# First attention of a hybrid block: two score buffers instead of three, four pairs of output banks instead of two, head weights applied after the normalisation, evictions issued ahead of exponents

## The reference

```python
logits = jnp.einsum('bhid,bhjd->bhij', q, k) * SCALE
logits = jnp.einsum('bhij,gh->bgij', logits, Wpre)
attn = jax.nn.softmax(logits, axis=-1)
attn = jnp.einsum('bhij,gh->bgij', attn, Wpost)
out = jnp.einsum('bhij,bhjd->bhid', attn, v)
```

## Time and profile before

| | |
|---|---|
| Median of 3 runs | 2481.05 us (2480.69 to 2481.33) |
| Profiled execution | 2480.47 us, its span 2478.7 us |
| Granted TensorE clock, mean over the span | 0.945 |
| Busy over the span | PE 89%, DVE 84%, ACT 74%, POOL 50% |
| First attention, first to last row maximum | 77.4 to 1488.9 us |
| 600 to 1000 us, busy | PE 387.36, DVE 368.22, ACT 347.33, POOL 191.12 us, PE clock 1.00 |

### The profile page before, as it was taken

How to read it: one execution, slowest core, us unless ns; L and a number is a source line. 1 busy time by engine, 2 the same in 40 slices (tenths; PEclk the granted TensorE clock), 3 DMA queues, 4 the chain that set the end, 5 groups by cost and what they waited for, 6 DMA issues and landing times. The chain is left out here.

```text
span 2478.7 us, 62316 instructions
## 1 busy us (share of the span) xinstructions
PE 2199.3 (89%) x22576; PEld 1502.2 (61%) x22576; DVE 2077.6 (84%) x3160; ACT 1822.4 (74%) x2674; POOL 1237.8 (50%) x1482
## 2 busy tenths in 40 slices
PE   5899999999999999999999994556899999999556
PEld 3466676666766676666766664443455555555544
DVE  6899999999999999999999995655799999997473
ACT  1788888888888888888888882115799998998002
POOL 3445444444444544445444452300788888887030
PEclk9999999999999999999999997669799999999866
DMA  2799999999999999999999993006222222222001
GB/s 93 121 196 187 196 187 192 191 192 189 194 189 194 184 197 192 190 189 192 192 189 191 192 194 71 1 8 207 70 69 72 70 69 70 70 69 51 29 1 34
DMA packets 1183691, 333.54 MB, mean 135 GB/s; under 512 B 1145968, under 2 KB 1174512, under 8 KB 1183216
## 3 DMA queue, kind: packets, MB, share of 16 engines
q1 hardware_dynamic: 1182320, 326.97, 74.2%
q10 hardware_dynamic: 1152, 3.62, 0.4%
HBM read 30.57 MB, written 14.68 MB: 18 GB/s over the span
## 5 line engine op out<-in xcount | busy, mean ns | idle before, releaser
L329 PE MATMUL a_out_ps<-a_vs,a_pT 128*128 128x129 f16 x4096 | 726.0, 221 | 48.4 <-ACT a_own_out L378 46.6
L416 DVE SCALAR_TENSOR_TENSOR a_parts<-a_probs,a_parts 128x1024 f16<-128x1024 f32 x512 | 653.2, 1276 | 115.1 <-ACT a_parts L369 115.1
L333 PE MATMUL a_out_ps<-a_vs,a_pT 128*128 128x129 f16 x4096 | 724.5, 219 | 0.0
L331 PE MATMUL a_out_ps<-a_vs,a_pT 128*128 128x128 f16 x4096 | 724.4, 218 | 0.0
L361 ACT ACTIVATE a_probs<-a_score_ps,a_negmax 128x1024 f32<-128x1024 f32 x512 | 571.8, 1117 | 164.9 <-DVE a_negmax L410 164.8
L410 DVE TENSOR_REDUCE a_negmax<-a_score_ps 128x1 f32<-128x1024 f32 x512 | 621.2, 1213 | 2.4 <-PE a_score_ps L315 2.4
L369 ACT ACTIVATE a_parts<-a_probs 128x1024 f16<-128x1024 f32 x512 | 543.5, 1061 | 0.6 <-DMA a_pT<-a_parts 0.6
L329 PEld LDWEIGHTS a_out_ps<-a_vs,a_pT 128*128 128x128 f16 x4096 | 396.4, 97 | 146.1 <-ACT a_own_out L378 99.1
L331 PEld LDWEIGHTS a_out_ps<-a_vs,a_pT 128*128 128x128 f16 x4096 | 402.9, 98 | 44.6
L477 POOL TENSOR_TENSOR acc<-acc,a_own_out 128x256 f32<-128x256 f32 x256 | 247.9, 969 | 352.3 <-DVE a_parts L416 346.4
L311 PE MATMUL a_score_ps<-kh,a_qs 128*128 128x512 f16 x1024 | 388.6, 379 | 10.3 <-DVE a_qs L401 7.0
(11 more groups left out here) (199 smaller groups left out, 2701.4 us busy)
## 6 DMA issues: line engine op xcount, KB each, us to landing
a_pT<-a_parts SPq DMA_TRANSPOSE x512, 5.0
b_qs<-q_parts SPq DMA_DIRECT2D x128, 64.0 KB, 2.0
b_ks<-k_parts SPq DMA_DIRECT2D x128, 64.0 KB, 1.9
q_parts<-b_parts SPq DMA_DIRECT2D x32, 128.0 KB, 1.9
k_parts<-b_parts SPq DMA_DIRECT2D x32, 128.0 KB, 1.9
v_parts<-b_v_all SPq DMA_DIRECT2D x4, 1024.0 KB, 4.6
b_vs<-v_parts SPq DMA_DIRECT2D x32, 128.0 KB, 2.1
b_sent_pT<-b_sent_parts SPq DMA_TRANSPOSE x256, 2.3
```

The costliest lines, as they stand in the source:

```text
L329: pe.matmul(out[:, 0:D + 1], hi, vs[:, G % 2, 0, j, 0:D + 1], start=j == 0, stop=False, skip_group_check=True)
L331: pe.matmul(out[:, 0:D], hi, vs[:, G % 2, 1, j, 0:D], start=False, stop=False, skip_group_check=True)
L333: last = pe.matmul(out[:, 0:D + 1], lo, vs[:, G % 2, 0, j, 0:D + 1], start=False, stop=j == JB - 1, skip_group_check=True)
L416: dve.scalar_tensor_tensor(out=parts[:, T % RING_P, 1, :], in0=probs[:, T % RING_P, :], scalar=PSCALE, in1=parts[:, T % RING_P, 0, :], op0 ...
```

## The change

Five things change in `attend_a`. The three score buffers become two, so `scores(T)` waits for the exponent of T - 2 in place of T - 3. The output banks go from two pairs to four, so `times_v(T)` waits for the eviction of tile T - 7 in place of T - 3. v is split into its parts once per batch instead of being scaled and split once per head, and POOL multiplies each evicted pair by `wpost` (`weigh`) and then adds it. ACT's `evict` stands ahead of the step's `exponentiate`, and DVE's `invert` ahead of its `row_max`. The addition of a pair follows the weighing of the next, and both stand at odd steps.

```diff
+        weighed = st.sb(s, "a_weighed", [P, 2, 2, D])
         qs = st.sb(s, "a_qs", [P, 2, 2, SEQ], F16)
-        vs = st.sb(s, "a_vs", [P, 2, 2, JB, D + 2], F16)
-        vtmp = st.sb(s, "a_vtmp", [P, JB, D])
-        score_ps = [st.ps(s, f"a_score_ps{i}", [P, SEQ]) for i in range(3)]
-        out_ps = st.ps(s, "a_out_ps", [P, 2, 2, 2 * D])
+        vs = st.sb(s, "a_vs", [P, NB, 2, JB, D + 2], F16)
+        score_ps = [st.ps(s, f"a_score_ps{i}", [P, SEQ]) for i in range(2)]
+        out_ps = st.ps(s, "a_out_ps", [P, 4, 2, 2 * D])
...
                 G, t = T // TPB, T % TPB
                 if t == 0:
                     pe.wait_ge(qlo_made, G + 1)
-                if T >= 3:
-                    pe.wait_ge(exp_done, T - 2)
-                out, base = score_ps[T % 3], G // HA * SEQ
+                if T >= 2:
+                    pe.wait_ge(exp_done, T - 1)
+                out, base = score_ps[T % 2], G // HA * SEQ
                 qhi, qlo = qs[:, G % 2, 0, t * P:(t + 1) * P], qs[:, G % 2, 1, t * P:(t + 1) * P]
...
             def times_v(T):
-                G, t = T // TPB, T % TPB
-                if t == 0:
-                    pe.wait_ge(vlo_made, G + 1)
-                if T >= 4 and T % 2 == 0:
-                    pe.wait_ge(evicted, T - 2)
+                b = T // (HA * TPB)
+                if T % (HA * TPB) == 0:
+                    pe.wait_ge(vlo_made, b + 1)
+                if T >= 8 and T % 2 == 0:
+                    pe.wait_ge(evicted, T - 6)
                 wait_turned(pe, T)
-                out = out_ps[:, T // 2 % 2, T % 2, :]
+                out = out_ps[:, T // 2 % 4, T % 2, :]
                 for j in range(JB):
                     hi, lo = pT[:, T % RING_T, 0, j, :], pT[:, T % RING_T, 1, j, :]
-                    pe.matmul(out[:, 0:D + 1], hi, vs[:, G % 2, 0, j, 0:D + 1], start=j == 0, stop=False,
+                    pe.matmul(out[:, 0:D + 1], hi, vs[:, b, 0, j, 0:D + 1], start=j == 0, stop=False,
-                    pe.matmul(out[:, 0:D], hi, vs[:, G % 2, 1, j, 0:D], start=False, stop=False,
+                    pe.matmul(out[:, 0:D], hi, vs[:, b, 1, j, 0:D], start=False, stop=False,
-                    last = pe.matmul(out[:, 0:D + 1], lo, vs[:, G % 2, 0, j, 0:D + 1], start=False,
+                    last = pe.matmul(out[:, 0:D + 1], lo, vs[:, b, 0, j, 0:D + 1], start=False,
                                      stop=j == JB - 1, skip_group_check=True)
                 last.then_inc(pv_done, 1)
...
                 act.wait_ge(max_ready, T + 1)
                 if T >= RING_P:
                     act.wait_ge(lo_ready, T - RING_P + 1)
-                act.activation(probs[:, T % RING_P, :], score_ps[T % 3][:], ACT.Exp,
+                act.activation(probs[:, T % RING_P, :], score_ps[T % 2][:], ACT.Exp,
                                bias=negmax[:, T % 8:T % 8 + 1]).then_inc(exp_done, 1)
             def high(T):
...
                 act.wait_ge(rden_ready, pair + 1)
                 if pair >= 2:
-                    act.wait_ge(added, pair - 1)
+                    act.wait_ge(weighed_ready, pair - 1)
                 for T in (2 * pair, 2 * pair + 1):
-                    act.activation(own_out[:, T % 4, :], out_ps[:, pair % 2, T % 2, 0:D], ACT.Copy,
+                    act.activation(own_out[:, T % 4, :], out_ps[:, pair % 4, T % 2, 0:D], ACT.Copy,
                                    scale=rden[:, pair % 2, T % 2:T % 2 + 1]).then_inc(evicted, 1)
             scale_q(0)
             scale_q(1)
             for i in range(TILES_A + AH + 2):
+                if i >= AH + 2 and i % 2 == 0:
+                    evict((i - AH - 2) // 2)
                 if i < TILES_A:
                     exponentiate(i)
-                if i >= AH + 2 and i % 2 == 0:
-                    evict((i - AH - 2) // 2)
                 if 1 <= i <= TILES_A:
                     high(i - 1)
                 if i % TPB == 1 and i < TILES_A:
...
                 dve.wait_ge(scored, T + 1)
                 if T >= 8:
                     dve.wait_ge(exp_done, T - 7)
-                dve.tensor_reduce(negmax[:, T % 8:T % 8 + 1], score_ps[T % 3][:], AX.X, ALU.max,
+                dve.tensor_reduce(negmax[:, T % 8:T % 8 + 1], score_ps[T % 2][:], AX.X, ALU.max,
                                   negate=True).then_inc(max_ready, 1)
             def low(T):
...
                 dve.wait_ge(pv_done, 2 * pair + 2)
                 if pair >= 2:
                     dve.wait_ge(evicted, 2 * pair - 2)
-                dve.reciprocal(rden[:, pair % 2, :], out_ps[:, pair % 2, :, D]).then_inc(rden_ready, 1)
+                dve.reciprocal(rden[:, pair % 2, :], out_ps[:, pair % 4, :, D]).then_inc(rden_ready, 1)
             low_q(0)
             low_q(1)
             for i in range(TILES_A + AH + 2):
+                if i >= AH + 2 and i % 2 == 0:
+                    invert((i - AH - 2) // 2)
                 if i < TILES_A:
                     row_max(i)
-                if i >= AH + 2 and i % 2 == 0:
-                    invert((i - AH - 2) // 2)
                 if 2 <= i < TILES_A + 2:
                     low(i - 2)
                 if i % TPB == 3 and TPB <= i < TILES_A:
...
                 if i >= 2:
                     pool.wait_ge(lo_ready, min(i - 1, TILES_A))
-            def scale_v(G, c):
-
-                if c == 0 and G >= 1:
-                    pool.wait_ge(vlo_made, G)
+            def high_v(b):
+
+                pool.tensor_scalar(vs[:, b, 0, :, 0:D], v[:, b * SEQ:(b + 1) * SEQ].rearrange("p (j d) -> p j d", j=JB),
+                                   1.0, 1.0, ALU.mult, ALU.mult).then_inc(vhi_made, 1)
+
+            def low_v(b, c):
+
+                pool.wait_ge(vhi_made, b + 1)
                 own = slice(c * JB // 2, (c + 1) * JB // 2)
-                src = v[:, (G // HA) * SEQ + c * HALF:(G // HA) * SEQ + (c + 1) * HALF]
-                w = wpost[:, (G % HA) * D:(G % HA + 1) * D][:, None, :].broadcast_to([P, JB // 2, D])
-                pool.tensor_tensor(vtmp[:, own, :], src.rearrange("p (j d) -> p j d", j=JB // 2), w,
-                                   ALU.mult).then_inc(v_scaled, 1)
-
-            def high_v(G):
-
-                pool.wait_ge(v_scaled, 2 * G + 2)
-                if G >= 2:
-                    pool.wait_ge(pv_done, TPB * (G - 1))
-                pool.tensor_scalar(vs[:, G % 2, 0, :, 0:D], vtmp[:], 1.0, 1.0, ALU.mult, ALU.mult).then_inc(vhi_made, 1)
-
-            def low_v(G, c):
-
-                pool.wait_ge(vhi_made, G + 1)
-                own = slice(c * JB // 2, (c + 1) * JB // 2)
-                last = pool.tensor_tensor(vs[:, G % 2, 1, own, 0:D], vtmp[:, own, :], vs[:, G % 2, 0, own, 0:D],
-                                          ALU.subtract)
+                src = v[:, b * SEQ + c * HALF:b * SEQ + (c + 1) * HALF]
+                last = pool.tensor_tensor(vs[:, b, 1, own, 0:D], src.rearrange("p (j d) -> p j d", j=JB // 2),
+                                          vs[:, b, 0, own, 0:D], ALU.subtract)
                 if c == 1:
                     last.then_inc(vlo_made, 1)
+            def weigh(pair):
+
+                pool.wait_ge(evicted, 2 * pair + 2)
+                if pair >= 2:
+                    pool.wait_ge(added, pair - 1)
+                g = 2 * pair // TPB % HA
+                w = wpost[:, g * D:(g + 1) * D][:, None, :].broadcast_to([P, 2, D])
+                slot = 2 * pair % 4
+                pool.tensor_tensor(weighed[:, pair % 2, :, :], own_out[:, slot:slot + 2, :], w,
+                                   ALU.mult).then_inc(weighed_ready, 1)
+
             def add(pair):
-                pool.wait_ge(evicted, 2 * pair + 2)
+                pool.wait_ge(weighed_ready, pair + 1)
                 at = (2 * pair // TPB // HA) * TPB + 2 * pair % TPB
-                slot = 2 * pair % 4
-                pool.tensor_tensor(acc[:, at:at + 2, :], acc[:, at:at + 2, :], own_out[:, slot:slot + 2, :],
+                pool.tensor_tensor(acc[:, at:at + 2, :], acc[:, at:at + 2, :], weighed[:, pair % 2, :, :],
                                    ALU.add).then_inc(added, 1)
             pool.memset(vs[:, :, 0, :, D:], 1.0).then_inc(ones_ready, 1)
+            high_v(0)
+            low_v(0, 0)
+            low_v(0, 1)
             pool.memset(acc[:], 0.0).then_inc(cleared, 1)
             pool.wait_ge(cleared, 1)
-            for i in range(TILES_A + AH + 4):
-                G, t = i // TPB, i % TPB
-                if i < TILES_A and t < 5:
+            for i in range(TILES_A + AH + 2):
+                b, step = i // (HA * TPB) + 1, i % (HA * TPB) - 3 * TPB
+                if b < NB and step in (0, 2, 4):
                     pace(i)
-                    if t in (0, 1):
-                        scale_v(G, t)
-                    elif t == 2:
-                        high_v(G)
+                    if step == 0:
+                        high_v(b)
                     else:
-                        low_v(G, t - 3)
```

(19 more changed lines are left out.)

## The result

The changed kernel takes 2453.45 us (median of 3 runs, 2450.41 to 2457.91), against 2481.05 before: a ratio of 0.989, 95% interval 0.987 to 0.991. It is 27.6 us faster. I had said 2435, 46 us faster, with 2425 to 2464 as the range. Its runs lie 7.5 us apart, where those of before lay 0.6 us apart.

A forecast was written before the change was run, and what follows sets the result against it. A DVE-ACT loop was taken to set the pace: 20.81 us plus 0.58 for POOL is 21.39 us a group, a gain of 0.76; times 62, less 2 us once, gives 45.1 off 2480.47: 2435 us, range 2425 to 2464.

The forecast's parts named there:

- my own forecast: The main case for the changed kernel: 21.28 to 21.55 us a group of eight tiles, 2423 to 2445 us; chance 0.52.
- full blocking: Rival: POOL and DVE fully block each other at low parts, 21.85 us a group, 2445 to 2464 us; chance 0.22.
- What bounds the kernel: A loop between DVE and ACT, not PE, sets the pace of about 22.15 us per group of eight tiles.
- Evictions and reciprocals ahead: ACT's and DVE's new order: no new wait for the reciprocal, 6.83 us through ACT, loop 20.81 us a group without POOL's effect.
- Weights on evicted outputs: POOL's weighing and adding slow DVE's low parts: 0.24 us at steps 6 and 8, 0.10 at step 4, 0.58 a group.
- Four output banks, two score buffers: PE's 0.70 us wait a group for evicted banks goes; neither part gains by itself, and score buffers leave no reserve.
- score buffers' rival: Score buffers bind: a late exponent 4 stalls PE each group, some 21.6 us a group, 2448 us; chance 0.12.
- Transposes: The DMA's landing of 5.0 us is hidden behind the about 7.8 us before a high part needs it.
- PE's floor: PE's own pace when left alone: 2.66 us a tile, 21.28 us a group.
- Once: One-time costs: third score's wait, v's parts beside the first `low_q`, one more POOL operation at the end; +2 us together.
- if high parts wait for DMAs: Sign of being wrong: ACT's high parts wait for the transposing DMAs; no size given.
- The two others: Signs of being wrong: score matmuls wait for exponents over 0.2 us a group; POOL's two operations take over 1.7 us a pair.

The follow-up runs named there:

- experiment 3: Only the banks changed (two score buffers, four pairs of output banks) on the kernel before: 2479.67 us, ratio 1.000.
- experiment 2: Only the order changed (evictions ahead of exponents, reciprocals ahead of row maxima) on the kernel before: 2545.15 us, ratio 1.027.
- experiment 4: Only v's parts made once per batch and the weights put on evicted outputs, on the kernel before: 2457.4 us, ratio 0.992.
- experiment 7: The changed kernel with only the high parts transposed, half the bytes per DMA: 2428.54 us, ratio 0.978, groups of 21.28 us.

## Why the prediction was right, and what was mis-sized

The time lies inside the stated range, and the direction and its cause were right. Yet 2453.45 us is above the 2423 to 2445 us of my own forecast and among the 2445 to 2464 us that I gave to full blocking, whose price didn't come (0.24 us, not 0.37). That the range held is in part luck: it reached up for a rival that was wrong, and covered a wait that I had put at nothing.

- *What bounds the kernel.* Right. The banks alone changed PE's wait and not the time (experiment 3); the DVE-ACT loop at 22.17 us decided.
- *Evictions and reciprocals ahead.* Right within this change: 6.84 against 6.83 us on the path through ACT, and the loop 21.21 against 21.39. It holds only together with the weights; alone the order costs 66 us (experiment 2), which my text did not see, since it priced the order as free of waits.
- *Weights on evicted outputs.* The price of 0.24 us per low part was right, at two places, and 0 instead of 0.10 at the third. I counted only its cost. Its gain, the wait for POOL and the 0.40 us at step 4 gone, was inside my sum of the new loop, but not named as the largest single part; it brings 22 us by itself (experiment 4).
- *Four output banks, two score buffers.* Nothing by themselves, as said. The score buffers' rival did not come: PE waits 3.8 us for exponents in 400 us, 0.2 us a group.
- *Transposes.* This is the term that was mis-sized. The prediction said "It is hidden unless landings reach the 7.4 us maximum often", and put 0 us. I compared one landing of 5.0 us with the 7.8 us that a slot allows. Landings stayed at 5.1 us. I left out that transposes run one behind the other on one queue, so that a transpose starts late when the queue is behind. The queue takes 2.71 us each in this kernel, against the 2.65 that the other engines have without it (experiment 7). With 21.67 us as the mean of 61 groups, from the first `low_q` in the loop to the last, that is (21.67 - 21.28) x 62 = 24 us.
- *PE's floor.* 21.28 us was right. I could neglect it beside a loop of 21.39; beside 21.21 it takes 0.07 x 62 = 4 us.
- *Once.* I put +2 for start and end together. The end of the stage cost 2.7 us, and the stages behind it, which the change doesn't touch, 2.0 more.

The sum, corrected: 47 us of the forecast's loop, 11 more since the loop was 0.18 us better (0.18 x 62), less 24 for the transposes and 4 for PE is 30 us in the groups, where 31.8 were measured. Less the 4.7 us behind the last row maximum it is 25 us, near the 27 of the spans.

Of the signs, the reciprocals and evictions fell as drawn: no wait for `own_out`, even low parts at 1.45 us. Row maxima are 2.70 us apart and not 2.66 to 2.68, and low parts behind `scale_q` still wait 1.14 us in some groups and 0.36 in others. Among the signs of being wrong, "if high parts wait for DMAs" came true, with 38.9 us. The two others came to their limits without a cost of their own that these runs show: 0.2 us a group for exponents, and 1.70 us as POOL's mean pair (965 and 731 ns), which counts its time held up behind `low_q`.

## What to carry to other kernels

When a loop between engines is shortened, every queue that turns once per step needs its own pace beside the new one. For a DMA queue that is the distance between issues while it is never idle, and not the time to landing; a queue that is behind shows it by starting later and later after its data is ready. A part of a change that pays in company can cost alone: moving an instruction forward moves its waits ahead of what now stands behind it. An engine's long wait is worth nothing until it is shown that others wait for that engine.

## What the runs showed of the hardware

A DMA transpose of a 128 x 2048 float16 tile took 2.49 us in a row alone, 2.73 us beside PE's instruction stream with nothing else running, and 2.98 us where PE went through its instructions faster. Half a tile took 1.47 us in the full kernel, where a whole one took 2.71, so cost doesn't halve with bytes. I had not expected that an engine's straight-line code takes time from a data queue that it has nothing to do with; 142 fetches of some 16 KB are only 2.33 of the kernel's 333 MB.
